# Second graph layer: the stages of a tile follow each other one tile closer, its product stands between two halves of another tile's MLP, and the logits go to another bank

## The reference, cut to what matters

```
xn = layernorm(x)                                      # x: 6250 nodes x 256
# SAGE layer: agg[n] = sum of rows x[src] over the edges with dst == n; mean = agg / max(count, 1)
h    = relu(mean(xn) @ W1l.T + b1 + xn @ W1r.T)
gnn  = mean(h) @ W2l.T + b2 + h @ W2r.T                # second layer: a new mean over the same edges
mix  = linear-attention block with its MLP, of xn      # shares its time with the first layer
x    = x + gnn + mix
# router of the expert MLP
H      = gelu(layernorm(x) @ W1 + b1)                  # 256 -> 1024
probs  = softmax(H @ Wg + bg)                          # 1024 -> 8 experts
out    = x + probs[e] * (H @ Wd[e] + bd[e])  for e = argmax(probs)
```

## Time and profile before

| | |
|---|---|
| median of 3 runs | 2472.18 us |
| span of the profiled execution | 2464.9 us |
| TensorE, VectorE, ScalarE, GpSimd busy | 1925.4, 1145.2, 561.3, 1692.3 us |
| gathers of layer 1, of layer 2 on GpSimd | 772.9 us busy, 750.1 us busy |
| first gather of layer 2, start of the last | 1124.3, 2112.0 us |
| first step of ranking after the last logits | 2147.57 us |

### The profile page before, as it was taken

How to read it: one execution, slowest core, us unless ns; L and a number is a source line. 1 busy time by engine, 2 the same in 40 slices (tenths; PEclk the granted TensorE clock), 3 DMA queues, 4 the chain that set the end, 5 groups by cost and what they waited for, 6 DMA issues and landing times.

```text
span 2464.9 us, 41722 instructions
## 1 busy us (share of the span) xinstructions
PE 1925.4 (78%) x9589; PEld 1194.8 (48%) x9590; DVE 1145.2 (46%) x3187; ACT 561.3 (23%) x1270; POOL 1692.3 (69%) x1759
## 2 busy tenths in 40 slices
PE   2599988888688877786899999877764543679998
PEld 1255555555355555553455555443332211368886
DVE  6444444434377777775655555443322221252221
ACT  5544433333122222221222222111110000101110
POOL 4577777777777777775777777777777777264442
PEclk9999999989799999987999999887876665789999
DMA  5444444444444444443455545454444333235551
GB/s 175 136 125 121 126 124 121 120 119 122 121 137 132 131 134 134 134 128 106 154 174 158 172 148 174 137 164 125 151 126 132 115 115 105 97 138 167 166 167 64
DMA packets 155421, 332.58 MB, mean 135 GB/s; under 512 B 35285, under 2 KB 89527, under 8 KB 155349
## 3 DMA queue, kind: packets, MB, share of 16 engines
q0 software_dynamic: 85824, 248.21, 34.4%
q10 hardware_dynamic: 42630, 58.35, 6.8%
q1 hardware_dynamic: 26898, 25.33, 3.3%
HBM read 273.97 MB, written 58.72 MB: 135 GB/s over the span
## 4 chain that ended last, share of the span: by engine, by line
POOL 34%; PE 28%; issue 16%; DVE 11%; DMA 3%; DVEq 3%; POOLq 2%; ACT 2%; SPq 0%; ACTq 0%
POOL big L686 34%; PE bank L526 8%; PE bank L1687 8%; PE bank L1455 4%; PE bank L1675 2%; DVE S L856 1%; DMA mbuf<-qT_d 1%; PE bank L1461 1%; DVE m_s L984 1%; POOLq L683 1%; PE bank L1610 1%; DVE m_t L978 1%; POOL big L696 1%; DVE res L1014 1%; PE bank L1485 1%
## 5 line engine op out<-in xcount | busy, mean ns | idle before, releaser
L686 POOL DMA_INDIRECT big<-xh_d,edges x782 | 772.9, 988 | 243.6 <-issue 231.3
L686 POOL DMA_INDIRECT big<-hh_d,edges x782 | 750.1, 959 | 256.9 <-issue 231.5
L1455 PE MATMUL bank<-big,S 128*128 x1960 | 591.1, 427 | 249.0 <-SPq L596 237.1
L856 DVE SCALAR_TENSOR_TENSOR S<-edges,tv,iota 128x512 f16<-128x512 f16 x490 | 365.2, 753 | 430.0 <-PE bank L1455 289.9
L1455 PEld LDWEIGHTS bank<-big,S 128*128 128x128 f16 x1960 | 204.1, 104 | 535.8 <-issue 393.0
L1453 PE MATMUL bank<-ones,S 128*128 128x1 f16 x980 | 166.8, 170 | 72.3 <-SPq L596 55.4
L526 PE MATMUL bank<-turned,x1T 128*128 128x512 f32 x392 | 194.4, 618 | 0.0
L707 POOL DMA_INDIRECT out_dram<-big,node_s x56 | 56.8, 1014 | 145.1 <-DVE big L1189 139.0
L1383 ACT ACTIVATE x1T<-bank 128x256 f32<-128x256 f32 x49 | 18.9, 385 | 527.9 <-PE bank L1461 527.8
L1453 PEld LDWEIGHTS bank<-ones,S 128*128 128x128 f16 x980 | 96.0, 98 | 86.9 <-SPq L596 67.3
L1189 DVE SCALAR_TENSOR_TENSOR big<-bank,prob_s,res 128x256 f32<-128x256 f32 x56 | 27.1, 484 | 179.3 <-PE bank L1689 179.3
(11 more groups left out here) (228 smaller groups left out, 2927.0 us busy)
## 6 DMA issues: line engine op xcount, KB each, us to landing
hx_d<-mbuf ACTq DMA_DIRECT2D x49, 512.0 KB
big<-xh_d,edges POOLq DMA_INDIRECT x782
big<-hh_d,edges POOLq DMA_INDIRECT x782
big<-in_fwd_dram SPq DMA_DIRECT2D x8, 1024.0 KB, 6.1
xh_d<-big SPq DMA_DIRECT2D x49, 128.0 KB, 2.2
qT_d<-abuf ACTq DMA_DIRECT2D x49, 128.0 KB
hh_d<-HL ACTq DMA_DIRECT2D x49, 128.0 KB
mbuf<-qT_d ACTq DMA_DIRECT2D x49, 128.0 KB
```

The source lines that it names most:

```text
L686: e.indirect_dma_start(G[:, r, n % SC, :], None, table, bass.IndirectOffsetOnAxis(ap=srcx[:, n:n + 1], axis=0)).then_inc(d_g[r], 16)
L856: VI.done(e.scalar_tensor_tensor(S[:, walk.u, :, :], dst[:, bass.ds(c * SC, SC)].unsqueeze(2).to_broadcast([P, SC, P]), tv[:, bass.ds(k, 1 ...
L1455: ins = e.matmul(AGG[:], S[:, walk.u, j, :], G[:, bass.ds(slot, 1), j, :].rearrange("p a c -> p (a c)"), start=False, stop=False, skip_gro ...
```

## The change

Each step of a turn works one tile closer to the tile that has just been summed. TensorE's order in a turn is now `trx(t-1)`, `hiddenT(t-2)`, `tr1(t)`, first half of `hidden(t-1)`, `out2(t)`, second half of `hidden(t-1)`, `logits(t-2)`. On VectorE `x2(t)` and `logits(t-2)` follow `mean_of(t)`. The logits are built in bank `CNT` in place of `B6`; `hiddenT` writes that bank too, and therefore waits for the copy of the logits of the tile before. `trx` no longer waits for a copy. Two draining turns are left in place of three. Besides, in all register arithmetic on the table's words `% 64`, `% 256` and `% 2` are written as masks, `& 63`, `& 255` and `& 1`, in both layers.

```
-                self.t, self.last = self.kept(self.w % 64, TILES - 1), None
+                self.t, self.last = self.kept(self.w & 63, TILES - 1), None
-                self.last = self.kept((self.w >> (6 + self.u)) % 2, 1)
+                self.last = self.kept((self.w >> (6 + self.u)) & 1, 1)
...
 # VectorE
                 def logits(t):
                     PL2.wait(e, "lg", t)
-                    VL2.done(e.tensor_copy(LG[...], B6[:, 0:NE]), "lg")
+                    VL2.done(e.tensor_copy(LG[...], CNT[:, 0:NE]), "lg")
...
-                    t = Turn(e, t, (0, 1, TILES + 2))
+                    t = Turn(e, t, (1, 2, TILES + 3))
                     mean_of(t)
-                    with e.If(t.base > 2):
-                        x2(t - 1)
-                        logits(t - 3)
-                    with e.If(t.base < 3):
-                        with e.If(t.base > 0):
-                            x2(t - 1)
-                        hold(e)
+                    x2(t)
+                    with e.If(t.base > 1):
+                        logits(t - 2)
...
-            for t in range(TILES, TILES + 3):
+            for t in range(TILES, TILES + 2):
 # ScalarE
-                part(e, t, 1, meanT)
-                part(e, t, 2, xT)
-                part(e, t, 3, hiddenT)
-                part(e, t, 2, hid)
+                part(e, t, 1, xT)
+                part(e, t, 2, hiddenT)
+                part(e, t, 0, meanT)
+                part(e, t, 1, hid)
                 part(e, t, 1, store)
 # TensorE
                 def trx(t):
                     VX2.wait(e, "xf", t)
-                    VL2.wait(e, "lg", t, 2)
...
                 def hiddenT(t):
+                    VL2.wait(e, "lg", t, 1)
...
-                    with e.If(t.base > 2):
-                        trx(t - 2)
-                        hiddenT(t - 3)
-                        out2(t - 1)
-                        hidden(t - 2)
-                        logits(t - 3)
-                        tr1(t)
+                    with e.If(t.base > 1):
+                        trx(t - 1)
+                        hiddenT(t - 2)
+                        tr1(t)
+                        hidden(t - 1, 0)
+                        out2(t)
+                        hidden(t - 1, 1)
+                        logits(t - 2)
```

More of the change, by code:

```diff
@@ L493, in __init__ @@
                 self.k = body * nu + first
-                self.set_counts(self.w % 256 + self.ready)
+                self.set_counts((self.w & 255) + self.ready)
             def set_counts(self, c):
@@ L1591, in trx, with hidden @@
                     VX2.wait(e, "xf", t)
-                    VL2.wait(e, "lg", t, 2)
                     PX2.done(transposes(B6, C, m_t), "tr")
-                def hidden(t):
-                    AT2.wait(e, "xT", t)
-                    for b in range(2):
-                        n = slice(b * 512, b * 512 + 512)
-                        if isinstance(t, int):
-                            AG2.wait(e, f"g{b}", t, 1)
-                        PG2.done(matmuls(e, pb[4 + b][:], [(ones3[:], fb1[:, b * 4:b * 4 + 4, :])] + [(x1T[:, h, :], fw1[:, h, n]) for h in range(CH)]),
-                                 f"h{b}")
+                def hidden(t, b):
+                    if b == 0:
+                        AT2.wait(e, "xT", t)
+                    n = slice(b * 512, b * 512 + 512)
+                    if isinstance(t, int):
+                        AG2.wait(e, f"g{b}", t, 1)
+                    PG2.done(matmuls(e, pb[4 + b][:], [(ones3[:], fb1[:, b * 4:b * 4 + 4, :])] + [(x1T[:, h, :], fw1[:, h, n]) for h in range(CH)]),
+                             f"h{b}")
                 def hiddenT(t):
+                    VL2.wait(e, "lg", t, 1)
                     for b in range(2):
@@ L1614, in logits @@
                     AH2.wait(e, "e1", t)
-                    if isinstance(t, int):
-                        VL2.wait(e, "lg", t, 1)
-                    PL2.done(matmuls(e, B6[:, 0:NE], [(HT[:, j, :], fwg[:, j, :]) for j in range(HJ)] + [(ones3[:], fbg)]), "lg")
+                    PL2.done(matmuls(e, CNT[:, 0:NE], [(HT[:, j, :], fwg[:, j, :]) for j in range(HJ)] + [(ones3[:], fbg)]), "lg")
                 def tr1(t):
```

35 lines of the change are left out of this document (19 added, 16 removed).

## The result

The changed kernel took 2566.7 us (median of four runs, 2564.5 to 2574.5), the kernel before 2472.0 in the same comparison: 1.039 times as long, 95% interval 1.037 to 1.041. The prediction was 2528 us, from 2488 to 2558. The direction and the place were as predicted, the size was not: +95 us instead of +56. The span of the profiled execution is 2566.4 us, and that execution took 2568.3 us, so only 1.9 us lie around it; the 7.3 us of the prediction compared a span with the median of other executions. Since all its sums are differences, this costs nothing.

A forecast was written before the change was run, and what follows sets the result against it. Layer 2 was taken as bound by GpSimd's gathers, with TensorE near to holding them. First turns 4 plus lag 74 minus slack 14.4 gave 64 us, less 8 at the end: +56, 2528 us, range 2488 to 2558.

The forecast's parts named there:

- the 7.3 us of the prediction: Whole kernel: the median of 2472.18 us was said to stand 7.3 us above the profiled span of 2464.9.
- The gathers bound layer 2, and TensorE was near to holding them: Layer 2: gathers set its length, GpSimd waiting 7.1 us for sums; no slack at tile 19; 40 to 90 us waits expected.
- The wait for the mean in mid-turn closes a loop through both engines: Layer 2 turns: 6.8 us copy to mean plus 8.2 behind it, 15.1 us, which is 2.25 us longer.
- Masks at nothing, bank at nothing: Masks: none taken per one-hot, bounds 0.2 us saved to 0.3 lost; layer 1 0, 3 us either way; no bank cost listed.
- Turns 1 to 4 add 4 us together: First turns of layer 2: 4 us lost together, between 0 and 9, since VectorE's other work bounds turn 4 anyway.
- The lag of 2.85 us per turn: Turns 5 to 30 of layer 2: 1.95 us plus 0.9 for the clock; 26 turns give 74 us.
- The clock was taken at 0.9 us: TensorE after each stall: a slower clock costs 0.9 us per turn, from a range of 0 to 2.0.
- The saving of 0.3 us on VectorE: VectorE, per turn: 0.2 us from a dropped compare-and-branch and jump, 0.1 from sums coming sooner.
- The third case of the prediction: Rival: the clock falls in every turn, lag 1.95 + 2.0 us, +84 us, 2557 us; chance 0.15.
- From tile 33 on nothing more is added: Late layer 2: a tile's gathers take longer than the longer turn, so no further loss; GpSimd's lost time is not given back.
- slack at tile 31: Layer 2 ring of slots: 14.4 us between a slot's release and its next gather, subtracted from the summed lag.
- The end, 7.8 us gained: Drain after the last mean, tile 48: no stall there, hiddenT of tile 48 starts at 2134.5 in place of 2142.34.

The follow-up runs named there:

- e2: Kernel before with the masks, and clearing and tr1 moved ahead of both halves of hidden, behind out2; 2527.6 us, ratio 1.024.
- e3: Changed kernel with clearing and tr1 moved behind the first half of hidden; 2496.7 us, 1.011 times the kernel before.
- e8: Changed kernel with three unread full-size products between hiddenT and the wait for the mean; 2534.0 us, 1.024 times the kernel before.
- e1: Kernel before with only the mask edits in the register arithmetic; 2466.6 us, ratio 0.999.
- e6: Changed kernel with the logits back in bank B6, hiddenT not waiting for their copy; first run 3360.2 us, beside 3048.4 of the kernel before.
- e11: Changed kernel without VectorE's splitting of the experts' bias in turn 4, two copies in its place; 3359.2 us beside 3049.1 of the kernel before.
- e12: Kernel before with the masks, without the splitting of the experts' bias in turn 4; 3144.3 us beside 3049.1 of the kernel before.
- e6b: Repeat, in another comparison, of the changed kernel with the logits back in bank B6; 2567.0 us, 1.038 times the kernel before.

## Why the prediction came out too low

- **The gathers bound layer 2, and TensorE was near to holding them**: right. GpSimd waited for sums 128.7 us in place of 7.1.
- **The wait for the mean in mid-turn closes a loop through both engines**: right, shown by e2 and e3, which move this step alone. The turn without the clock's price (15.1 us) came out to a tenth of a us once e8 had kept the clock up, in both its parts.
- **Masks at nothing, bank at nothing**: right within 0.2 us per turn (e1, e6). Layer 1 gained 4.5 us, just outside the 3 either way that were given; e1, with no other edit, gained 7.4. In the nine traces with the masks, one execution each, the first gather of layer 2 starts at 1116.6 to 1121.1, so 3 to 8 us sooner, and the difference between these two is scatter.
- **"Turns 1 to 4 add 4 us together"**: the largest wrong size, 28 us in its place. The mean of tile 5 starts 1229.8 - 1119.8 = 110.0 us behind the first gather, before it was 81.7 (worked out from the same two starts, 1206.0 and 1124.3). The prediction gave a reason for turn 4 alone: VectorE's other work "bounds turn 4 anyway". But 15 of the 28 us are there before it: the mean of tile 3 starts 67.4 us behind the first gather in place of 52.2 (rows below). In turns 0 to 2 VectorE now stands for 2.98, 4.04 and 6.18 us until out2 of the same tile is done, then does its layer norm, and only then the next one-hots; before there was no x2 in turn 0, and those of turns 1 and 2 stood for 1.10 and 0.30 us. From the mean of tile 3 to that of tile 4, where VectorE splits the experts' bias, 5.6 us more are added, and from there to the mean of tile 5 7.5. In turn 4 TensorE did its whole turn under VectorE's work before, and only clearing and tr1 were left behind the mean; now nearly the whole turn comes behind it, 10.4 us from the end of the mean to the next items (rows below), where clearing and tr1 alone are 0.6. e2 and e1 divide the 28 us. e2 has the old order in its first three turns and the early wait from turn 3 on: its mean of tile 3 comes at 54.2 us (e1 53.5) and that of tile 5 at 97.6 (e1 83.7). So 14 us belong to the early wait in turns 3 and 4 and 2 to the masks, and the other 12, by difference, to the order one tile closer, in turns 0 to 2. Which part of that order it is was not taken apart, and e11, which was to take the split away, gave no usable time.
- **The lag of 2.85 us per turn**: the second wrong size. The turn grew by 16.5 - 12.8 = 3.7 us; over 25 turns from tile 5 to 30 that is 92 us, where 2.85 gives 71. Two of its terms were off. The clock was taken at 0.9 us, "below the middle", and cost 1.4 (e8): 13 us over the 25 turns. It fell in 19 of the 25 turns, behind stalls as short as 1.48 us, so "a stall of 1.4 us may leave the clock alone" did not carry the low value. The saving of 0.3 us on VectorE did not come at all (e8's turn is 15.1 us and not 14.8): 8 us. The bounds of 0 to 2.0 us for the clock held. The third case of the prediction (it falls in every turn, 2557 us) was the nearest, but by two opposite errors: 3.95 us per turn, above what was measured, and 4 us for the first turns. The terms behind the mean add to 8.3 us as they are printed there and to 15.1 for the turn; the 8.2 beside them is a matter of rounding.
- **"From tile 33 on nothing more is added"**: held. 28 + 92 + one more turn of 3.7 - 14.4 of slack at tile 31 = 109 us (the two sizes as measured), and the gathers were held by 111.9. Counted from the first gather, the mean of tile 31 came 541 us in place of 417, and that of tile 41 737 in place of 622: turns of five and six items grew as well, but the delay shrank from 124 to 115 us, as the slack was used up.
- **The end, 7.8 us gained**: 6.7. There was no stall, as predicted.

The first turns on VectorE, the kernel before: x2 of turns 1 and 2 and the mean of tile 3.

```profile
1159.34 0.42 DVE L1047 TENSOR_TENSOR res<-res,bank 128x256 f32 x1 [1.10 <-PE bank L526]
...
1167.59 0.42 DVE L1047 TENSOR_TENSOR res<-res,bank 128x256 f32 x1 [0.30 <-issue]
...
1176.51 0.48 DVE L874 SCALAR_TENSOR_TENSOR mean<-bank,RC,lo 128x256 f32<-128x256 f32 x1
```

The changed kernel: x2 of turns 0, 1 and 2 and the mean of tile 3.

```profile
1147.91 0.42 DVE L1047 TENSOR_TENSOR res<-res,bank 128x256 f32 x1 [2.98 <-PE bank L526]
...
1162.07 0.42 DVE L1047 TENSOR_TENSOR res<-res,bank 128x256 f32 x1 [4.04 <-PE bank L526]
...
1176.72 0.42 DVE L1047 TENSOR_TENSOR res<-res,bank 128x256 f32 x1 [6.18 <-PE bank L526]
...
1187.17 0.48 DVE L874 SCALAR_TENSOR_TENSOR mean<-bank,RC,lo 128x256 f32<-128x256 f32 x1
```

Turn 4 in the timeline of the changed kernel: end of the bias work, mean, clearing, next items.

```profile
1209.99 0.68 DVE L848 CAST w<-big 3x1024 bf16<-3x1024 f32 x1
...
1213.64 0.48 DVE L874 SCALAR_TENSOR_TENSOR mean<-bank,RC,lo 128x256 f32<-128x256 f32 x1
...
1214.18 0.60 PE L1437 MATMUL bank<-zero 1*128 1x512 f16 x1 [11.72 <-DVE mean L874]
...
1224.49 1.69 PE L1452 MATMUL bank<-big,S 128*128 x7
```

By the prediction's own sum with the two sizes put right, 109 - 7 - 4.5 = +98 us stands beside a measured difference of spans of 101.5.

## What to carry to other kernels

When a wait is moved to an earlier place on a full engine, price it as a loop: from the event that starts the late engine, through it, through the wait, and through all that now stands behind the wait, back to that event. Price the first turns by themselves, since the loop can bind there where the steady turns say nothing of it: here they cost 28 us of the 124 that were lost up to tile 31. Look too for the turn in which the late engine does extra work, since the whole turn behind the wait is exposed there. A stall of 2 us in each turn costs more than itself when the clock falls behind it: carry that price as a range, for it was 1.4 us per turn with stalls of some 1.9 us and 0.7 with stalls of 1.2 (e2).

## What the runs showed of the hardware

- Stalls of some 1.9 us in each turn brought the granted clock to 0.90 over 335 us, and cost 1.4 us per turn of 16.5 beside the stall (e8 against the changed kernel). The clock fell in 19 of 25 turns; in e2, with stalls of 1.2 us, in 11 of 25.
- Twelve one-row products of zeros in the stall kept TensorE recorded as busy for most of it and did nothing for the clock (0.90); three full f32 products in the same place brought it to 0.98. Rows, type and values differ together, so which of them matters is open.
- A gather that starts while VectorE builds a one-hot ends 0.81 to 0.83 us after the one-hot, however long that still runs (341 gathers in six traces, 0.20 to 0.68 us to go), so it takes up to 1.5 us instead of 0.95. One that starts within some 0.05 us of the one-hot's start is not held. A changed order on VectorE made 150 of 782 longer than 1.1 us instead of 23 to 37, and cost 26 us.
- In three comparisons the kernel before took 3048 to 3115 us, 23 to 26% more. The clearest pair is one and the same kernel (e6 and e6b, 3360.2 and 2567.0 us): VectorE's one-hots waited for nothing that the profile shows for 616.5 us in 264 places, 20.9 at the longest, against 139.5 us, 195 and 1.8 (rows below), while both executions moved the same bytes. All kernels with other loop code fell behind the kernel before by 3% and more there, e12 too (3144.3 us), whose nearest relative e1 had been even with it. The cause stays open.

The waits of e6, then of e6b, one row each (us in total, times, longest):

```profile
DVE S L856 <- issue: 616.5, 264, 20.9
...
DVE S L856 <- issue: 139.5, 195, 1.8
```
